# A perceiver block on one core: one of four tiles of probabilities is turned by VectorE over DRAM instead of by TensorE

## What is computed

```python
q = (x @ w_q).reshape(B, Sq, 16, 64).transpose(0, 2, 1, 3)
k = (context @ w_k).reshape(B, 257, 16, 64).transpose(0, 2, 1, 3)
v = (context @ w_v).reshape(B, 257, 16, 64).transpose(0, 2, 1, 3)
sim = jnp.einsum('bhid,bhjd->bhij', q, k) * SCALE
attn = jax.nn.softmax(sim, axis=-1)
out = jnp.einsum('bhij,bhjd->bhid', attn, v)
return out.transpose(0, 2, 1, 3).reshape(B, Sq, 1024) @ w_o + b_o
```

## Time and profile before

| | us |
|---|---|
| median of 3 runs (lowest to highest) | 1586.78 (1586.59 to 1586.93) |
| the profiled execution | 1586.93 |
| its span, first to last instruction | 1585.0 |

### The profile page before, as it was taken

One profiled execution on the slowest core, in us unless ns is written; L12 is line 12 of the kernel. 1 busy time (PEld: TensorE's weight loads), 2 busy tenths in 40 slices (PEclk: granted clock), 3 DMA queues, 4 the chain that ended last, 5 costly groups with the idle time before them and its releaser, 6 DMA issues. The chain is left out here.

```text
span 1585.0 us, 30386 instructions
## 1 busy us (share of the span) xinstructions
PE 1569.8 (99%) x11114; PEld 1377.5 (87%) x11114; DVE 1245.0 (79%) x2409; ACT 1021.1 (64%) x2025; POOL 822.0 (52%) x784
## 2 busy tenths in 40 slices
PE   9999999999999999999999999999999999999998
PEld 7889899898999989999899888988988887888886
DVE  6558878887888878878788685767777889989887
ACT  3457777777777777777787442445446666666765
POOL 3318657376573856747456242333334555555554
PEclk9999999999999999999999999999999999999999
DMA  8984636456364654635433684432436601011010
GB/s 253 271 258 150 180 111 189 127 169 176 117 185 120 178 164 128 187 108 152 139 112 95 186 284 137 136 90 81 139 96 222 244 14 61 20 36 39 7 54 27
DMA packets 203412, 215.60 MB, mean 136 GB/s; under 512 B 83776, under 2 KB 149632, under 8 KB 203264
## 3 DMA queue, kind: packets, MB, share of 16 engines
q1 hardware_dynamic: 203264, 213.66, 43.8%
HBM read 154.88 MB, written 58.72 MB: 135 GB/s over the span
## 5 line engine op out<-in xcount | busy, mean ns | idle before, releaser
L79 PE MATMUL p_bank_score<-p_ctxt,p_qo 128*128 128x256 f32 x2304 | 304.6, 286 | 0.8 <-ACT p_probs L1112 0.4
L79 PEld LDWEIGHTS p_bank_score<-p_ctxt,p_qo 128*128 128x128 f32 x2304 | 288.1, 191 | 5.9 <-issue 2.2
L79 PE MATMUL p_bank_mix<-p_probt,p_ctx 128*128 128x512 f32 x1152 | 292.0, 397 | 0.5
L79 PEld LDWEIGHTS p_bank_mix<-p_probt,p_ctx 128*128 128x128 f32 x1152 | 207.4, 189 | 41.8 <-issue 3.8
L1316 DVE SCALAR_TENSOR_TENSOR p_qo<-p_bank_mix,p_odd,p_qo 128x512 fp32r<-128x512 f32 x192 | 143.8, 749 | 57.6 <-ACT p_qo L1126 50.1
L1126 ACT ACTIVATE p_qo<-p_bank_mix,p_odd 128x512 fp32r<-128x512 f32 x192 | 132.4, 690 | 68.2 <-PE p_bank_mix L79 67.6
L1112 ACT ACTIVATE p_probs<-p_bank_score,p_small 128x257 f32<-128x257 f32 x256 | 121.5, 475 | 58.6 <-DVE p_small L1297 54.1
L801 POOL TENSOR_SCALAR p_probs<-p_probs,p_small 128x256 f32<-128x256 f32 x256 | 122.2, 485 | 68.9 <-DVE p_small L1303 68.8
L795 POOL TENSOR_TENSOR p_ctx<-p_ctx_in,p_ctx 128x768 fp32r<-128x768 f32 x64 | 118.5, 1851 | 66.7 <-ACT p_ctx L1101 66.4
L790 POOL TENSOR_TENSOR p_ctx_in<-p_ctx_in,p_odd_in 128x768 f32<-128x768 f32 x64 | 118.2, 1847 | 40.2 <-DMA p_odd_in<-in_ctx_dram 40.2
L1297 DVE TENSOR_REDUCE p_small<-p_bank_score 128x1 f32<-128x257 f32 x256 | 105.4, 415 | 10.2 <-PE p_bank_score L79 7.6
(11 more groups left out here) (302 smaller groups left out, 3917.4 us busy)
## 6 DMA issues: line engine op xcount, KB each, us to landing
p_blocks_in<-in_ctx_dram SPq DMA_DIRECT2D x256, 96.0 KB, 2.4
p_ctx_in<-in_ctx_dram SPq DMA_DIRECT2D x64, 384.0 KB, 3.1
q<-p_ctx SPq DMA_DIRECT2D x64, 256.0 KB, 3.7
ffn<-p_w_raw SPq DMA_DIRECT2D x64, 256.0 KB, 2.9
p_odd_in<-in_ctx_dram SPq DMA_DIRECT2D x64, 192.0 KB, 3.6
p_x<-in_x_dram SPq DMA_DIRECT2D x32, 256.0 KB, 4.1
p_quad<-q SPq DMA_DIRECT2D x32, 256.0 KB, 3.6
p_probt<-q SPq DMA_DIRECT2D x32, 256.0 KB, 3.8
```

The costliest lines, as they stand in the source:

```text
L79: made = e.matmul(out, lhsT, rhs, start=n == 0, stop=n == last)
```

## The change

`is_moved(b)` is true for batches 1 to 6 of each group of eight. In those, the first of the four tiles of probabilities takes another way:

- GpSimd's `scale` writes it, its columns regrouped, to `moving` (a place that `probt`'s low half uses later), after waiting for the last mix that read that place.
- SyncE stores it to the DRAM tensor `p` (`put_rows`), and later loads it back in four transfers with its 32x32 blocks exchanged (`move_blocks`).
- In the next batch, VectorE turns the 32x32 blocks (`turn_moved`), ScalarE makes the high part (`high_moved`), GpSimd the low part (`low_moved`).
- TensorE's `turn_probs` leaves out this tile's two transposes, and `high_probs` and `low_probs` of the first half work on one tile instead of two.
- `mix` adds its products in another order (all that need the high part of `probt` first), and waits for the low part only ahead of the last two of the first piece.
- SyncE's order changes: `load_context` and `load_odd` come last in a batch, behind the blocks and the moved tile.
- VectorE's `invert(b, 0)` comes ahead of `top(b, 1)`, and `turn_moved` between them.

```diff
+        def is_moved(b):
+
+            return 0 < b % GB < GB - 1
+        def moved_from(b):
+            return moving[b % 2][:, 0, 2 * P:2 * P + KEYS]
+        def moved_to(b):
+            return probs[b * NT % 6][:, 0:KEYS]
+        def turned_to(b):
+            return moving[b % 2][:, :, 0:P]
...
+            def put_rows(b):
+                e.wait_ge(normal, b * NT + 1)
+                e.dma_start(p_dram[b % 2], moved_from(b)).then_inc(rows_put, DMA)
+
+            def move_blocks(b):
+                e.wait_ge(rows_put, DMA * moves(b))
+                for q in range(NQD):
+                    e.dma_start(moved_to(b)[q * QUAD:(q + 1) * QUAD, :].rearrange("r (h n) -> r h n", h=HT),
+                                p_dram[b % 2, :, q * SP * QUAD:(q + 1) * SP * QUAD].rearrange(
+                                    "(h r) n -> r h n", r=QUAD)).then_inc(blocks_moved, DMA)
...
-                    if b + 2 < B:
-                        load_context(b + 2)
+                    if is_moved(b):
+                        put_rows(b)
                     for j in ffn_block_of(b + 1) if b % GB == 0 else ffn_block_of(b) if b % GB > 1 else ():
                         load_ffn_block(j)
                     if b + 2 < B:
                         if b % GB > 0:
                             load_blocks(b + 2)
+                    if is_moved(b):
+                        move_blocks(b)
+                    if b + 2 < B:
+                        load_context(b + 2)
                         load_odd(b + 2)
...
-                e.tensor_scalar(probs[n % 6][:, 0:KEYS], probs[n % 6][:, 0:KEYS], small[n % 4][:, 2:3], 1.0,
-                                ALU.mult, ALU.mult).then_inc(normal, 1)
+                to, made = probs[n % 6][:, 0:KEYS], probs[n % 6][:, 0:KEYS]
+                if tile == 0 and is_moved(b):
+                    e.wait_ge(mixed, KC * (b - 1))
+                    to = moved_from(b).rearrange("p (q s k) -> p s q k", s=SP, k=QUAD)
+                    made = made.rearrange("p (s q k) -> p s q k", s=SP, k=QUAD)
+                e.tensor_scalar(to, made, small[n % 4][:, 2:3], 1.0, ALU.mult, ALU.mult).then_inc(normal, 1)
+
+            def low_moved(b):
+                e.wait_ge(moved_hi, moves(b))
+                e.tensor_tensor(probt[b % 2][:, LO, :, 0:P], turned_to(b), f32(probt[b % 2][:, HI, :, 0:P]),
+                                ALU.subtract).then_inc(moved_lo, 1)
...
                 for tile in range(NT):
+                    if tile == 1 and is_moved(b - 1):
+                        low_moved(b - 1)
...
-                for i in range(2):
+                for i in (1,) if half == 0 and is_moved(b) else (0, 1):
...
-                    e.wait_ge(probt_lo, 2 * (b + 1))
+                    e.wait_ge(probt_hi, 2 * (b + 1))
+                    if is_moved(b):
+                        e.wait_ge(moved_hi, moves(b))
...
-                accumulate(e, b_mix[m], [x for s in range(SP) for x in three(
-                    lambda h, s=s: ctx[i][:, h, s, cols], lambda h, s=s: probt[i][:, h, s, :])]
-                ).then_inc(mixed, 1)
+                for h in (HI, LO):
+                    for s in range(SP):
+                        e.matmul(b_mix[m], ctx[i][:, h, s, cols], probt[i][:, HI, s, :], start=h == HI and s == 0,
+                                 stop=False)
+                if m == 0:
+                    e.wait_ge(probt_lo, 2 * (b + 1))
+                    if is_moved(b):
+                        e.wait_ge(moved_lo, moves(b))
...
+            def high_moved(b):
+                e.wait_ge(blocks_turned, moves(b))
+                e.activation(probt[b % 2][:, HI, :, 0:P], turned_to(b), ACT.Copy).then_inc(moved_hi, 1)
...
+            def turn_moved(b):
+                e.wait_ge(blocks_moved, DMA * NQD * moves(b))
+                e.transpose(turned_to(b).rearrange("p s (h r) -> p h s r", r=QUAD),
+                            moved_to(b).rearrange("p (h s k) -> p h s k", s=SP, k=QUAD)).then_inc(blocks_turned, 1)
...
                             low_probs(b - 1, 1)
+                        if is_moved(b - 1):
+                            invert(b, 0)
+                            turn_moved(b - 1)
                         top(b, 1)
-                        invert(b, 0)
+                        if not is_moved(b - 1):
+                            invert(b, 0)
```

More of the change, by code:

```diff
@@ L307, in cross_attention @@
             ctxt = [carve(second, f"ctxt{i}", [P, 2, KC, KEYS], F32R) for i in range(2)]
+            with ExitStack() as between:
+                carve(between, "probt0_high", [P, SP, ROW])
+                moving = [carve(between, "moving0", [P, SP, ROW])]
             probt = [carve(second, "probt0", [P, 2, SP, ROW], F32R)]
+            with ExitStack() as between:
+                carve(between, "probt1_high", [P, SP, ROW])
+                moving.append(carve(between, "moving1", [P, SP, ROW]))
             with ExitStack() as boundaries:
@@ L374, in probs_bank, with moves, probs_rows @@
             return b_probt
+        def is_moved(b):
+            return 0 < b % GB < GB - 1
+        def moves(b):
+            return b // GB * (GB - 2) + b % GB
+        def moved_from(b):
[4 more added lines that the diff above has]
+            return moving[b % 2][:, :, 0:P]
         FIRST_TWO = [(b, 1 + 4 * b) for b in range(2)]
+        def probs_rows(b, half, side):
+            first = P if half == 0 and is_moved(b) else 0
+            return (probt[b % 2][:, side, :, half * 2 * P + first:(half + 1) * 2 * P],
+                    probs_bank(b, half).rearrange("p (s r) -> p s r", s=SP)[:, :, first:2 * P])
         def turned_in(b):
@@ L410, in cross_attention @@
             "probs_turned", "probt_hi", "probt_lo", "mixed", "out_hi", "out_lo")
+        rows_put, blocks_moved, blocks_turned, moved_hi, moved_lo = room.sems(
+            "rows_put", "blocks_moved", "blocks_turned", "moved_hi", "moved_lo")
         queried, qo_hi, qo_lo, qo_mid, qo_pool, valued, o_half, o_whole = room.sems(
@@ L1106, in exponent @@
                     e.wait_ge(probs_turned, (n - 6) // 2 + 1)
+                if n >= 6 and (n - 6) % NT == 0 and is_moved((n - 6) // NT):
+                    e.wait_ge(blocks_turned, moves((n - 6) // NT))
                 if tile == 0 and b > 0 and b % GB == 0:
@@ L1308, in low_probs @@
                     e.wait_ge(o_gone[0], DMA * NT // 2 * (b // GB))
-                hi, lo = (probt[b % 2][:, s, :, half * 2 * P:(half + 1) * 2 * P] for s in (HI, LO))
-                e.tensor_tensor(lo, probs_bank(b, half).rearrange("p (s r) -> p s r", s=SP), f32(hi),
-                                ALU.subtract).then_inc(probt_lo, 1)
+                if half == 1 and is_moved(b):
+                    e.wait_ge(rows_put, DMA * moves(b))
+                (hi, bank), (lo, _) = (probs_rows(b, half, s) for s in (HI, LO))
+                e.tensor_tensor(lo, bank, f32(hi), ALU.subtract).then_inc(probt_lo, 1)
+            def turn_moved(b):
+                e.wait_ge(blocks_moved, DMA * NQD * moves(b))
+                e.transpose(turned_to(b).rearrange("p s (h r) -> p h s r", r=QUAD),
+                            moved_to(b).rearrange("p (h s k) -> p h s k", s=SP, k=QUAD)).then_inc(blocks_turned, 1)
             def low_mix(b, m):
```

15 lines of the change are left out of this document (11 added, 4 removed).

## The result

The change made the kernel slower: 1605.11 us median of 4 runs (1604.04 to 1608.97) against 1586.78; the ratio is 1.012 [1.0105, 1.0135]. The profiled execution took 1605.84 us with a span of 1604.0. The forecast of 1577.3 was wrong in its sign; rival 1 named the mechanism, at too small a price (1598).

The account below looks back on a forecast made before the run. TensorE, busy 9.34 of 9.34 us a batch, was taken as the bound. From the profiled 1586.93, minus 10.5 for transposes plus 1.0 given back by SyncE gave 1577.4, or 1577.3 against the median; range 1575.3 to 1591.

Parts of the forecast that it names:

- rival 1: SyncE becomes the bound: low-part store takes 4.2 us, loop 9.9 us, 1598; slower 0.22, shared with a very late moved tile.
- SyncE's closed loop: SyncE's queue, low store to next low store in weight-block batches: 9.3 us, 0.15 over 9.12, about 1 us given back.
- The landing: Weight block's low-part store in SyncE's loop: taken as 3.6 us, behind 576 KB instead of 192 KB.
- The issues: SyncE's loop besides the landing: load 0.47, blocks 1.96, moved tile 1.96, context 0.4, odd row 0.54, high store 0.34 us.
- The number of turns: SyncE's loop was counted in 4 batches of each of 8 groups, 32 batches.
- the slack: Lateness of SyncE's loop absorbed before it costs time: 0.45 us a group, 3.6 us in all.
- the gain of 10.5 forecast: TensorE's queue: 96 transposes fewer at 0.109 us each, 10.5 us saved; moved batches go from 9.34 to 9.12 us.
- Rival 2: Moved tile's loads land late, at 3.3 to 3.4 us; VectorE and TensorE wait, no change at 1587; chance 0.14 with neighbours.
- Rival 3: TensorE: a transpose group's cost is largely changing over, so half the gain, 5 us, 1582; chance 0.08.
- The mix order: TensorE's mix products in another order: taken as 0, with 0 to 2 us either way.
- VectorE, ScalarE, GpSimd hidden: Added work fits beside TensorE's 9.12 us batch: VectorE busy 7.8, GpSimd 8.5, ScalarE +0.35 on 7.14.
- The 0.27 us that were left for VectorE: Tile 1's scaling, slipped by VectorE's 0.34 us, ends at 551.15; TensorE wants it at 551.42, leaving 0.27 us.

Follow-up runs that it names:

- high_between_six: Changed kernel with weight buffers swapped at each block, high part's store ahead of context and odd row, and no moved tile in the last group: 1580.8 us, ratio 0.9968.
- after_no_weights: Changed kernel with no weight block loaded, split or stored in the batches; raw weights copied in DRAM at groups' ends instead: 1581.53 us, ratio 0.9967.
- stores_first: Changed kernel with context and odd row issued just behind the two weight stores instead of just ahead of them: 1598.96 us, ratio 1.0074.
- all_three: Changed kernel with blocks exchanged on the way out, context and odd row behind the weight stores, swapped weight buffers, last group not moved: 1592.07 us, ratio 1.0031.
- ctx_first: Changed kernel with the context's rows loaded where they were before, ahead of the scaled tile's store: 1600.19 us, ratio 1.0082.
- before_ctx_last: Kernel before with only SyncE's order changed, the context's rows behind the blocks, no new issue: 1586.88 us, ratio 1.0.

## Why the prediction was wrong

**The step that failed** is SyncE's closed loop: "I take 3.6 us and a loop of 9.3 ... about 1 us given back". The loop and its members were listed rightly, and the 576 KB ahead of the stores as what would stretch it. The mechanism was right, then, and its sizes were not:

- *The landing.* 3.6 was assumed; from the low store to the load that waits for it 3.93 was measured in the median, 3.99 in the mean.
- *The issues.* All else in the loop was put at 5.7 us; a turn without a long issue has about the same (9.67 - 3.93), but with the long ones in 12 of 25 turns the mean is 6.3.
- *The number of turns.* The forecast counted 4 in each of 8 groups, 32. There are 32 weight blocks, 5 in each of six groups and 2 in the seventh, so 25 turns, and none in the last group. This was off to the other side.

With a mean turn of 10.28 instead of 9.3, over 25 turns and less the slack, that is 25.7 us given back instead of 1. Without the long issues it would have been 25 x 0.55 - 3.2 = 11 us, an estimate: the gain of 10.5 forecast eaten, and a little more than the 7.5 found. So the plain turn alone would have made the change useless; the long issues make most of the loss. Measured against the profile of before, the span is 19.0 us longer where 9.5 less was forecast.

**Rival 1** was right on mechanism and on its place; its 1598 rested on a loop of 9.9 in 32 turns. It gave the landing of 3.9 as the point of decision, which is what was measured; what it lacked are the long issues.

**Rival 2** did not happen. The moved tile's loads landed in 1.9 us, under the 2.4 assumed, and VectorE waited 4 times for them in 48. The Trainium skill ("DMA: Bandwidth & Descriptors", Specifications) wants runs of 512 bytes or more for line rate; the 32 KB loads in 256-byte runs show no landing above that of the 96 KB ones here, and no run sets short runs against long ones of equal size.

**Rival 3** did not either: in a batch without waits two transposes less give 9.34 - 9.11 = 0.23 us by the windows, 0.21 by the repeated distance of the maxima (9.33 to 9.12), so 0.105 each against 0.109 forecast.

**The mix order** at 0: right, 1586.66 by itself.

**VectorE, ScalarE, GpSimd hidden**: right in the first seven groups once the loop is open: `high_between_six` keeps all their work and has most batches at 9.10 to 9.13. In the changed kernel it did not hold for GpSimd, whose splitting waits for the late weight block and holds up the context's low part; the forecast took the block to be there. In the **last group** it was wrong in any case. There VectorE also splits output weights, which the prediction did not look at:

```profile
858.16 0.68 DVE L579 TENSOR_TENSOR p_wo_early<-p_w_raw,p_wo_early 128x512 fp32r<-128x512 f32 x1
858.76 0.42 DVE L1373 TENSOR_REDUCE p_small<-p_bank_score 128x1 f32<-128x257 f32 x1
```

The first maximum comes 2.18 us after the first scores (856.58), not 1.59 as in the changed kernel's batch above (568.79 against 567.20). The 0.27 us that were left for VectorE don't cover these 0.59, and a moved batch takes 9.49 to 9.51 where it took 9.33 (no run takes the splitting away alone). The last group has +0.7 us, where -1.3 was counted on. `high_between_six` leaves it unmoved.

**The forecast for the idea itself** was near, on the high side: with the loop opened, 1580.8 against 1577.3, and 7.5 us within the groups of `after_no_weights` against 10.5. What is missing are the batches at the start of a group (9.88 to 9.72 only), the last group, and in `high_between_six` a few batches of 9.2 to 9.8.

Open: why some issues take 1.1 to 1.7 us; why executions of the changed kernel differ by 5 us where those of before differ by under 2; and how the landing would be at other amounts ahead of it.

## What to carry to other kernels

A queue that issues in order and contains a wait for its own earlier transfer is an engine with a period: add up from that transfer's issue to its next one, landing included, and compare it with the period that you hope for, not with the present one. Count how many turns there really are. Take landing and issues at their means with the long ones in, for a loop without slack keeps every delay: here the loss followed the mean turn of 10.28 us, not the plain one of 9.67. And look what hangs on each transfer in the loop, on every engine. When a repair opens the loop, look which one through the same queue is next. The cheapest repair was neither fewer transfers nor faster ones, but to wait for the store that goes out early.

## What was not expected of the hardware

A store's landing went with what was issued straight before the pair of stores: 256 KB landed in a median of 2.1 us with no context and no odd row ahead (`stores_first`; 2.4 in `all_three`), 3.1 behind the odd row's 192 KB (before; 3.4 in `ctx_first`), and 3.7 to 4.2 behind 576 KB (the changed kernel and eight more; 4.0 in `before_ctx_last`, where the two stores stand as far apart as before). Issues of SyncE that mostly take 0.43 to 0.5 us take 1.1 to 1.7 now and then, whatever the transfer (1.38 for the first of the blocks at 575.97); in the changed kernel that befell 12 of 25 turns. And four copies of the same pieces from DRAM to DRAM took 2.46 to 3.63 us to issue, where the four loads took 1.88.
